# Attention and mixture-of-experts kernel on one Trainium2 core: the first LayerNorm moved from token rows to feature partitions

## What is computed

```python
def _layernorm(x, axis=-1, eps=1e-05):
    m = jnp.mean(x, axis=axis, keepdims=True)
    v = jnp.var(x, axis=axis, keepdims=True)
    return (x - m) / jnp.sqrt(v + eps)
...
    q = (x @ w_q) ...; k = (context @ w_k) ...; v = (context @ w_v) ...   # 16 heads of 64, blocks of 128 tokens
    attn = softmax(q k^T / 8)
    return (attn v) @ w_o + b_o
...
    x = x + xattn(_layernorm(x), ctx, w_q, w_k, w_v, w_o, b_o)
    x = x + ffn(_layernorm(x), gate, W1, b1, W2, b2)   # 8 experts, hidden 512, the best 2 by gate
```

## Time and profile before

| | us |
|---|---|
| median of 3 runs (1580.43 to 1581.63) | 1580.46 |
| the profiled execution | 1580.22 |
| its span, first to last instruction | 1578.5 |

### The profile page before, as it was taken

How to read it: one execution, slowest core, us unless ns; L and a number is a source line. 1 busy time by engine, 2 the same in 40 slices (tenths; PEclk the granted TensorE clock), 3 DMA queues, 4 the chain that set the end, 5 groups by cost and what they waited for, 6 DMA issues and landing times.

```text
span 1578.5 us, 45424 instructions
## 1 busy us (share of the span) xinstructions
PE 1553.8 (98%) x14150; PEld 1454.0 (92%) x14151; DVE 1176.1 (75%) x3796; ACT 1108.0 (70%) x3357; POOL 818.1 (52%) x946
## 2 busy tenths in 40 slices
PE   8999999999999999999999999999999999999997
PEld 7899999999899999999999989998899999999997
DVE  4777777777777777777777777777788777777775
ACT  5677677677776777767767777676666676777774
POOL 2344545545554554554555455455456555555556
PEclk9999999999999999999999999999999999999999
DMA  6522111222111221211122211122799755555554
GB/s 201 145 72 74 60 60 60 77 90 72 62 60 60 67 94 66 74 60 60 63 75 89 74 60 60 60 67 81 241 231 249 144 86 85 89 86 90 84 84 61
DMA packets 105643, 145.05 MB, mean 92 GB/s; under 512 B 12736, under 2 KB 87616, under 8 KB 105344
## 3 DMA queue, kind: packets, MB, share of 16 engines
q1 hardware_dynamic: 60144, 89.00, 17.8%
q0 software_dynamic: 26816, 37.32, 13.7%
q10 hardware_dynamic: 18640, 18.19, 4.4%
HBM read 77.09 MB, written 67.38 MB: 92 GB/s over the span
## 4 chain that ended last, share of the span: by engine, by line
issue 47%; POOL 22%; PE 9%; DVE 7%; DMA 6%; DVEq 3%; ACT 2%; POOLq 2%; ACTq 1%; SPq 0%
POOL lists L662 7%; DMA out<-stage_room,number 6%; PE bank_a L1404 4%; POOL prob L669 3%; DVE hid L1332 3%; POOL rstd L648 2%; DVE stage_room L1349 2%; POOL stage_room L711 2%; POOL stage_room L707 2%; POOL out L735 2%; DVEq L1344 1%; PE bank_v L1437 1%; POOLq L729 1%; PE bank_s L1422 1%; DVEq L1323 1%
## 5 line engine op out<-in xcount | busy, mean ns | idle before, releaser
L669 POOL TENSOR_TENSOR prob<-prob,inv 128x512 f32<-128x512 f32 x256 | 271.4, 1060 | 520.3 <-DVE inv L956 519.6
L777 ACT ACTIVATE prob<-bank_s,low 128x128 f32<-128x128 f32 x1024 | 363.3, 376 | 40.9 <-DVE low L951 40.9
L735 POOL DMA_INDIRECT out<-stage_room,number x142 | 231.8, 1632 | 53.9 <-issue 53.1
L951 DVE TENSOR_REDUCE low<-bank_s 128x4 f32<-128x512 f32 x256 | 175.4, 685 | 98.0 <-PE bank_s L1422 97.9
L777 ACT ACTIVATION_READ_ACCUMULATOR prob<-bank_s,low 128x1 f32 x1024 | 221.1, 216 | 0.0
L770 ACT ACTIVATE probt<-bank_t 128x512 f32<-128x512 f32 x256 | 153.4, 599 | 89.6 <-PE bank_t L1411 89.6
L1050 DVE SCALAR_TENSOR_TENSOR stage_room<-xin,wo_t 128x256 f32<-128x256 f32 x480 | 178.8, 426 | 0.0
L807 ACT ACTIVATE ot_h<-bank_v 128x512 fp32r<-128x512 f32 x128 | 77.4, 604 | 138.4 <-PE bank_v L1437 138.4
L885 ACT ACTIVATE hidt_h<-hid 128x512 fp32r<-128x512 f32 x142 | 89.7, 632 | 117.4 <-DVE hid L1332 112.2
L1411 PE MATMUL bank_t<-ident,prob 128*128 128x128 f32 x1024 | 161.9, 281 | 4.0 <-POOL prob L669 4.0
L1404 PE MATMUL bank_a<-xt_l,wq_h 128*128 128x256 f32 x512 | 152.4, 298 | 0.3 <-DVE xt_l L966 0.3
(11 more groups left out here) (231 smaller groups left out, 4728.9 us busy)
## 6 DMA issues: line engine op xcount, KB each, us to landing
stage_room<-lists ACTq DMA_DIRECT2D x67, 265.0 KB
halves<-stage_room SPq DMA_DIRECT2D x32, 512.0 KB
homes<-halves SPq DMA_DIRECT2D x16, 1024.0 KB, 6.4
xin<-in_x SPq DMA_DIRECT2D x32, 256.0 KB, 2.8
stage_room<-in_x SPq DMA_DIRECT2D x32, 256.0 KB
stage_room<-in_w SPq DMA_DIRECT2D x32, 256.0 KB, 4.3
out<-stage_room SPq DMA_DIRECT2D x32, 256.0 KB, 2.2
cin<-in_ctx SPq DMA_DIRECT2D x32, 128.0 KB, 2.6
```

The costliest lines, as they stand in the source:

```text
L669: pool.tensor_tensor(prob[:, n % 4, :, :], prob[:, n % 4, :, :], wide(inv[:, n % 4, :], P), ALU.mult).then_inc(s_norm.sem, 1)
L735: pool.indirect_dma_start(out, bass.IndirectOffsetOnAxis(ap=number[:, u, b:b + 1], axis=0), ysum[:, u, b, :], None, compute_op=ALU.add).th ...
L777: e = act.activation(prob[:, n % 4, h, :], bank_s[n % 2][:, h * P:(h + 1) * P], ACT.Exp, bias=low[:, n % 4, h:h + 1], scale=-1.0, accum_ou ...
L951: dve.tensor_reduce(low[:, n % 4, :], bank_s[n % 2][:, :].rearrange("p (h k) -> p h k", h=4), AX.X, ALU.min).then_inc(s_low.sem, 1)
```

## The change

The tokens also come transposed from the host (`x_t`, features by tokens). The load of a pair reads its slice into a new buffer `xraw` (features on partitions). The statistics are still made from `xin` by VectorE and GpSimd. The means and inverse deviations (two numbers for a token) are then written to a small DRAM tensor `ln_rows` and read back into `ln_all`, the same 512 numbers on all partitions (`ln_through`, SyncE). GpSimd subtracts and multiplies in slot 2, behind the norm of unit 2 (`normalise`, two instructions of 128 x 512). ScalarE makes the high part in slot 4 ahead of the exponentials, VectorE the low part in slot 4. "t0", its bank, `xn` and the instruction that wrote it go. The second two scatters move from slot 2 to slot 3, behind the norm of unit 3. The reciprocal of unit 3 moves from slot 4 to the end of slot 3, and three gate scores move from slot 3 into slots 1 and 2, which now have 8 and 6. With 15 products in a turn the banks are given by name (`BANK_OF`). In the first turn TensorE spreads the statistics by matmuls and VectorE normalises (`first_statistics`, `normalise_first`).

```diff
-        [("o1", FROM0), ("t0", NEXT)],
+        [("o1", FROM0)],
...
+    BANK_OF = {"q10": 0, "k10": 1, "o0": 2, "k11": 3, "q11": 0, "o1": 1, "v10": 2, "v11": 3,
+               "q00": 0, "k00": 1, "q01": 2, "k01": 3, "v00": 1, "f0": 0, "v01": 2}
...
+            def ln_through(sp, it):
+                if not isinstance(it, int) or it > 0:
+                    sp.wait_ge(ln_in, it * 16)
+                wait(sp, pool_step, it, "rstd1")
+                sp.dma_start(ln_rows, mean_var[:, 0, :, :]).then_inc(ln_out, 16)
+                sp.wait_ge(ln_out, it * 16 + 16)
+                wait(sp, xn_step, it - 1, "xn")
+                sp.dma_start(ln_all.rearrange("p t b k -> p (t b k)"), ln_rows.rearrange("t b k -> (t b k)").rearrange(
+                    "(o n) -> o n", o=1).to_broadcast([P, 4 * P])).then_inc(ln_in, 16)
...
+                    sp.dma_start(xraw.rearrange("p c b t -> p c (b t)"),
+                                 x_t[:, cols].rearrange("(c p) t -> p c t", p=P)).then_inc(xt_in, 16)
...
-                        wait(sp, ln1_step, it - 1, "ln1")
+                        wait(sp, xa_lo, it - 1, "x")
+                        wait(sp, ln1_step, it - 1, "bn1_1")
...
+                def of_tokens(k):
+                    return ln_all[:, :, :, k].rearrange("p t b -> p b t").rearrange(
+                        "p (o b) t -> p o b t", o=1).to_broadcast([P, DC, 2, P])
+                def normalise(it):
+                    pool.wait_ge(xt_in, (it + 2) * 16)
+                    pool.wait_ge(ln_in, it * 16 + 16)
+                    pool.tensor_tensor(xraw[:, :, :, :], xraw[:, :, :, :], of_tokens(0), ALU.subtract).then_inc(xn_step.sem, 1)
+                    wait(pool, xn_step, it, "centred")
+                    pool.tensor_tensor(xraw[:, :, :, :], xraw[:, :, :, :], of_tokens(1), ALU.mult).then_inc(xn_step.sem, 1)
...
-                        if n in (1, 2) and has(it - 1, PREV):
-                            send(it - 1, n - 1)
+                        if n == 2 and has(it, NEXT) and not (isinstance(it, int) and it < 0):
+                            normalise(it)
+                        if n in (1, 3) and has(it - 1, PREV):
+                            send(it - 1, n // 2)
...
+                        if n == 4 and has(it, NEXT):
+                            wait(act, a_full, it, "q11")
+                            wait(act, xn_step, it, "xn")
+                            act.activation(xt[0][:, 0:DC, :], xraw.rearrange("p c b t -> p c (b t)"),
+                                           ACT.Copy).then_inc(xa_hi.sem, 1)
                         if has(it, CUR):
                             exps(it, n)
...
+                def low_of_tokens(it):
+                    wait(dve, xa_hi, it, "x")
+                    dve.tensor_tensor(xt[1][:, 0:DC, :], xraw.rearrange("p c b t -> p c (b t)"),
+                                      xt[0][:, 0:DC, :].bitcast(F32), ALU.subtract).then_inc(xa_lo.sem, 1)
...
-                X_SCORES = {1: (0, 5), 2: (5, 6), 3: (11, 3), 5: (14, 2)}
+                X_SCORES = {1: [(0, 8)], 2: [(8, 3), (11, 3)], 5: [(14, 2)]}
...
-                        if n > 0 and has(it, of):
+                        if n not in (0, 4) and has(it, of):
                             inverse(it, name, n - 1)
...
+                        if n == 4 and has(it, NEXT):
+                            low_of_tokens(it)
...
-                            normalise(it, 0, xin, [xn[:, 0, :], xn[:, 1, :]])
...
+                        if n == 3 and has(it, NEAR[4][1]):
+                            inverse(it, NEAR[4][0], 3)
...
-                        if k == 0:
-                            wait(pe, a_done, it if g == 0 else it - 1, "t0")
+                        if name == "q00":
+                            wait(pe, xa_lo, it, "x")
```

More of the change, by code:

```diff
@@ L71, in wait, with program @@
         engine.wait_ge(signal.sem, value - back)
-def program(nc, x, ctx, w_all, w_ot, b_o, b_oc, gate, gate_t, w12, b1, b2, out):
+def program(nc, x, x_t, ctx, w_all, w_ot, b_o, b_oc, gate, gate_t, w12, b1, b2, out):
     tokens, D = x.shape
@@ L130, in program @@
         [("o1", FROM0)],
-        [("t0", NEXT), ("v10", CUR), ("v11", CUR)],
+        [("v10", CUR), ("v11", CUR)],
         [],
@@ L225, in program @@
             cin = place("cin", 2, 2 * P)
-            xn = place("xn", 2, D)
-            place("not_used", WORK + HOME - taken_to[0])
+            xraw = place("xraw", DC, 2, P)
+            ln_all = place("ln_all", P, 2, 2)
+            assert taken_to[0] == WORK + HOME
             qt = place("qt", 2, CHUNKS // 2, 2 * P)
@@ L359, in by_products, with a_bank @@
                 return isinstance(it, int) and it < 1
[L361 to L367, removed]
+            def a_bank(name):
+                return bank_a[BANK_OF[name]]
             def bank_before(it, name):
+                same = [n for n, _ in A_EVENTS if BANK_OF[n] == BANK_OF[name]]
                 if not isinstance(it, int):
[L372 to L376, removed]
+                    k = same.index(name) - 1
+                    return (it if k >= 0 else it - 1), same[k]
+                order = [(j, n) for j in range(-1, PAIRS + 1) for n in a_full.present(j) if n in same]
+                k = order.index((it, name)) - 1
                 return order[k] if k >= 0 else (it, None)
@@ L437, in program @@
             T_EARLY, T_ENDS, T_ALL = 23, 24, 48
-            bank_at = {name: a_bank(PAIRS, name) for name in ("o0", "o1", "f0")}
+            bank_at = {name: a_bank(name) for name in ("o0", "o1", "f0")}
             PLACES_AT = 5
             bank_h, bank_y = [bank_s, [bank_at["o0"], bank_at["o1"]]], [bank_t, bank_v]
-            bank_first = a_bank(PAIRS - 1, "v11")
+            bank_first = a_bank("v11")
             assert len({id(bank) for bank in (bank_first, *bank_at.values())}) == A_BANKS
@@ L958, in second_part @@
                 def second_part(it, name):
-                    src = a_bank(it, name)
+                    src = a_bank(name)
                     kind, k = name[0], int(name[-1])
[L961 to L968, removed]
+                    wait(dve, a_full, it, name)
+                    if kind == "v":
                         last = dve.tensor_copy(vv[:, int(name[1]), k, :], src[:, :])
@@ L1035, in rows_of @@
                     dve.wait_ge(sent, (it - 1) * 64 + 16)
-                    normalise(it, 1, x1, [rows[:, b, 0:D] for b in range(2)])
+                    normalise(it, x1, [rows[:, b, 0:D] for b in range(2)])
                 def x_scores(it, first, many):
@@ L1128, in body @@
                             wait(dve, ln1_step, it, "bn1_1")
[L1129 to L1130 removed]
+                            if not isinstance(it, int) or it > 0:
+                                dve.wait_ge(ln_out, it * 16)
+                            elif it == 0:
+                                dve.wait_ge(ln_first, 1)
                         name, of = NEAR[n]
[L1132 removed]
+                        if n not in (0, 4) and has(it, of):
                             inverse(it, name, n - 1)
                         if n == 1 and has(it, NEXT):
[L1135 removed]
+                            aggregate(it, 0)
                         if n == 4 and has(it, PREV):
[L1137 removed]
+                            aggregate(it, 1)
                         if n == 5 and has(it, PREV):
@@ L1365, in _ @@
                 after_step(PAIRS, "bn2_1")
-                aggregate(1)
+                aggregate(PAIRS, 1)
                 x_part(1, 1)
@@ L1567, in keep_busy, with first_statistics @@
                                   skip_group_check=True)
+                def first_statistics():
+                    wait(pe, pool_step, -1, "rstd1")
+                    pe.wait_ge(made, 20)
+                    for k in range(2):
+                        for b in range(2):
+                            last = pe.matmul(bank_s[1][:, (2 * k + b) * P:(2 * k + b + 1) * P],
+                                             mean_var[:, 0, b, k:k + 1].to_broadcast([P, P]), ident[:, :],
+                                             start=True, stop=True, skip_group_check=True)
+                    last.then_inc(ln_first, 1)
                 def gate_means():
@@ L1587, in _ @@
                 keep_busy(3)
-                pe.wait_ge(made, 20)
+                first_statistics()
                 iterations(pe, body)
```

65 lines of the change are left out of this document (37 added, 28 removed).

## The result

| | median us | runs | profiled span us |
|---|---|---|---|
| before, same chip | 1580.43 | 9 | 1578.5 (the profile ahead of the prediction) |
| after | 1584.77 (1583.93 to 1587.35) | 9 | 1583.9 |

The ratio is 1.0031, 95% interval 1.0021 to 1.0041: the change costs 4 to 5 us. The forecast was 1580.4 and no measurable change. The time lies inside the range, but the direction was missed.

The account below looks back on a forecast made before the run. TensorE was taken as the bound, busy 984.35 of 985 us. From 1580.22: -13.2 + 30 x 0.40 + 1.15 = -0.05; with the median 0.24 above the profile, forecast 1580.4 us, no measurable change, range 1570 to 1595.

Parts of the forecast that it names:

- rivals 2: GpSimd's inverse deviation, or from T = 1.79 unit 3's norm, holds VectorE's low parts in slot 4: about 1592; chance 0.31.
- Rival 3: Statistics return late from DRAM at 5 us a transfer, ScalarE 0.7 late: 1601; also T of 2.6, 39 us; chance 0.07.
- "t0" is worth 0.44: TensorE between "o1" and "w0": dropping the transposes saves 0.44 us a turn, 13.2 us over 30 turns.
- The chain in slot 4: ScalarE's later high part delays VectorE's low parts, so "k00" waits 0.35 us, 0.40 with a 0.05 block by GpSimd.
- What is next? ... 0.25 of cover: Unit 5's exponentials end at S + 8.18, slot 6's scores are due at S + 8.43: no further cost.
- The scatters a slot later: GpSimd's second scatters behind unit 3's norm: VectorE's idle ahead of slot 6 absorbs them; cost 0, at most 0.3.
- The start, +1.15: First turn: 0.65 us for 256 KB of `x_t` ahead of the weights, about 0.5 for `xt_h` in slot 4.
- T = 1.30: Length in us of each of GpSimd's two normalising instructions in slot 2; ScalarE allows up to 1.94.
- Rival 1: Slot 4's chain is not last and k00 doesn't wait: the whole 13.2 comes out, 1568.4 us; chance 0.20.

Follow-up runs that it names:

- Experiment 2: Changed kernel with VectorE making the context's low part ahead of the copy of v11 in slot 4: 1582.25 us, ratio 1.0004 to the kernel before.
- experiment 4: Kernel before the change with the second two scatters of a turn in slot 3 instead of slot 2: 1585.02 us, ratio 1.0025.
- experiment 5: Changed kernel with the second scatters left in slot 2, behind the two normalising instructions: 1604.9 us (one run).
- experiment 8: Changed kernel with ScalarE's high part ahead of the copy, last turn's second scatters in slot 2, first statistics ahead of three waiting matmuls: 1568.15 us, ratio 0.9921.
- experiment 7: Changed kernel with the statistics written to DRAM so that means and inverse deviations each lie without gaps: 1785.87 us (one run).
- experiment 1: Changed kernel with ScalarE's tokens' high part ahead of the copy of unit 2's probabilities in slot 4: 1570.18 us, ratio 0.9927 to the kernel before.

## Why the prediction was wrong

The direction was wrong, the main mechanism right. The prediction's own chances were even between slower (0.38) and same (0.37), but of the causes that it gave for slower, rivals 2 and 3, neither appeared. Step by step:

- **"t0" is worth 0.44**: right, 0.44 by the rows, not the 0.60 of its own row.
- **The chain in slot 4**: right to 0.02 us for all three starts. The wait of k00, forecast 0.40, is 0.41, but by luck: 0.05 of it was a block by GpSimd that didn't come, and the reaction of TensorE was undersized by nearly 0.1. I put k00 0.06 us behind the end of the context's low part; the rows give 630.80 - 630.65 = 0.15. Behind the wait another 0.06 is lost up to the scores, which the sum lacks. So a turn costs 0.47 instead of 0.40: 2.1 us over 30 turns, enough to turn -0.04 a turn into +0.04.
- **"What is next? ... 0.25 of cover"**: right. The last instruction of the exponentials (632.58, 0.21 us) ends at S + 8.16, forecast 8.18. Experiment 2 shows a reaction of 0.15 behind it (8.29 to 8.44), so the scores could have started at S + 8.31 and started at 8.55. The reaction, which I had left out, and the longer turn cancel.
- **The scatters a slot later, "I take 0, at most 0.3"**: this is the step that failed. Alone it costs 0.25% (experiment 4), almost as much as the whole change. I had reasoned only for a steady turn, where it holds (+0.02). I hadn't asked it of the last turn, where nothing is normalised and TensorE waits for norms: there it costs 2.2 us in the kernel before, 2.3 in the changed one (experiment 5) and 2.8 in its better version (experiment 8). The one turn with the pause, seen as 35.02 and passed over as an exception, grew by 0.8 and 1.0 us in the two kernels with late scatters, within what it varies by anyway.
- **The start, +1.15**: +2.03 between the two profiles, but -0.83 in experiment 5, whose start is the same program. So its size is not known, nor whether the +1.15 was wrong. I had named the 256 KB load; the first weights came only 0.15 us later (7.73 against 7.58). In the changed kernel's profile VectorE was later: `xn` before (5.96 to 6.95) filled a wait for weights, whereas the two instructions that replace it stand at 9.25 and 9.98, because TensorE must spread the statistics first, here at its slow pace; then the clock fell.
- **T = 1.30**: measured 1.62. By its own condition ScalarE waits only from 1.94, and it didn't wait. The Trainium skill's rule on steps above 8 bytes ("GPSIMD Engine Reference", "Performance pitfalls for Q7 kernels") has the right sign: 1.34 at a step of 4 bytes, 1.62 at 16 (experiment 7). That is 21% for a product with two inputs where one has the step of 16 bytes, not 50%.
- **Rival 1** (all of the 13.2 comes out) was false for this kernel, but experiment 1 reached it: 1570.
- **Rival 2** (the block) got the sign of the result and not its reason. T of 1.62 lay at its edge, and in the trace the inverse deviation (629.80, 0.72 us) does begin ahead of the context's low part (629.97, 0.68 us): neither is longer than alone, where the rival's formula gives a block of 2 x 1.62 - 2.55 = 0.69 us.
- **Rival 3** (late statistics): the cover, taken as 2.3 us, was 2.9. The two landings were 1.4 and 4.2 us, not 2.8 each.

So the term of the scatters and the turn's 0.47 are enough for the sign. What stays open: how much the start costs, as said above; why GpSimd pauses 3.4 to 5.0 us before one scatter, the 112th of 128 in all ten profiles, and why the length varies. No run was made on it.

## What to carry to other kernels

Where one engine is full, work taken off it is worth what the instructions behind it gain, and the new producer's place in its own queue decides whether anything is left. Here the same high part 0.8 us earlier in ScalarE's queue was worth about 15 us: ahead of a copy that was itself waiting, it moved that copy by 0.2 us and TensorE not at all. Moving a step "to a slot with room" must be asked of the first and the last turn too; they lack the work that hides it in the others. When a prediction comes down to 0.05 us a turn, the reaction times decide it, and they must be read from a row on the waiting engine, not from another one. And a difference between two profiles in a stretch that runs once is worth only as much as that stretch repeats: here the start of one program came out 2.9 us apart.

## What the runs showed of the hardware

- TensorE resumes 0.15 us after the end of the VectorE or ScalarE instruction it waits for (630.65 to 630.80; 563.05 to 563.20 in experiment 2), and lost about 0.06 more behind the first of these; ScalarE and VectorE answer each other in 0.03 to 0.04 us.
- VectorE and GpSimd don't hold each other both ways in every case. A VectorE instruction with two SBUF inputs that comes first holds a tiny GpSimd step: in experiment 2 the first step of the deviation took 0.72 instead of 0.20 us beside the context's low part, and the earlier trace rows showed 1.23 for the second one. But when GpSimd's power step of 128x2 had begun first, the VectorE instruction ran at its usual 0.68 us. The Trainium skill ("SBUF — State Buffer", "Who interferes with whom") has an exclusive lock, with the order of issue deciding who blocks; the first case agrees, this one doesn't. Nor was it free in experiment 1: the tokens' low part began 0.30 us before the end of a norm (584.83, 1.04 us) and took 0.85 instead of 0.69. All this was read from steady turns only, not measured apart.

```profile
559.64 0.72 POOL L663 TENSOR_TENSOR shifted<-mean_var,eps 128x2 f32<-128x2 f32 x1
```

- A write of 2 KB to DRAM landed in 1.4 us (median) in pieces of 16 bytes, and the issue that waited for it came 1.4 to 3.1 us behind the write's; in pieces of 4 bytes it came 8.5 to 11.3 us behind.
- The same eight matmuls in the first 10 us of one program took 1.92 us in one profile and 1.06 in another, and the granted clock reads 1.00 around both. From 30 to 48 us it was 0.81 in the one and 0.91 in the other.
- GpSimd pauses 3.4 to 5.0 us before the 112th of its 128 scatters of this kind, in each of ten profiles, with no releaser.
